# One fused kernel on one core: the output projection in three products of split parts, the mask counted ahead of the context, and a new order for every engine

## The reference, cut to what matters

```python
# L0: a routed low-rank update; lora_A is the context, 4 matrices of 64 rows
w     = softmax(x @ router_W.T + router_b)
a_sum = einsum('bsh,arh->bsr', x, lora_A)
x     = nan_to_num(x + 0.5 * einsum('bsn,bsnh->bsh', w, einsum('bsr,nhr->bsnh', a_sum, lora_B)))
# L1: cross attention, 32 heads of 16, over the 64 context rows; masked rows are left out
Q, K, V = x @ Wq.T + bq, ctx @ Wk.T + bk, ctx @ Wv.T + bv
scores   = where(mask != 0, Q K / 4, -inf)
attn_out = (softmax(scores) @ V) @ Wo.T + bo        # "the output projection"
x = layernorm(x + attn_out) * ln_g + ln_b
# L2 and L3, the same function: the 8 nearest of 512 columns, then 4 blocks
for i in range(4):
    p = leaky_relu(x); g = p gathered at the 8 neighbours
    x = (W_i @ p + (W_i @ g).sum(neighbours)) / 9 + x
```

## Time and profile before

| | us |
|---|---|
| median of 3 runs | 396.26 (395.89 to 396.88) |
| the profiled execution's own time | 396.18 |
| its span in the trace | 394.4 |
| PE busy | 379.3 (96%) |
| DVE busy | 274.2 (70%) |
| ACT busy | 173.8 (44%) |
| POOL busy | 122.8 (31%) |

### The profile page before, as it was taken

The page is one execution under the profiler, slowest core; times in us unless marked ns, Lnnn a source line. Parts: engine busy times, 40 slices in busy tenths (PEclk is TensorE's granted clock), DMA queues, the critical chain, the costliest instruction groups (busy, mean ns, idle before and its releaser), DMA issues.

```text
span 394.4 us, 6512 instructions
## 1 busy us (share of the span) xinstructions
PE 379.3 (96%) x2396; PEld 306.0 (78%) x2396; DVE 274.2 (70%) x410; ACT 173.8 (44%) x297; POOL 122.8 (31%) x116
## 2 busy tenths in 40 slices
PE   8899997998999989999999999999999999999996
PEld 7567786863976666666768988998899889988995
DVE  3968749689269874573779988785768564667764
ACT  1375438465467845454444433433433342333421
POOL 7560030210020313041413574452445231343420
PEclk9999999999999999999999999999999999999999
DMA  7994113407235303500000000000000001000012
GB/s 199 322 354 141 55 39 93 90 2 175 60 107 136 69 7 74 134 2 0 2 1 2 2 0 2 0 2 0 2 1 2 0 2 53 2 0 2 0 55 106
DMA packets 25199, 22.60 MB, mean 57 GB/s; under 512 B 9553, under 2 KB 20689, under 8 KB 25169
## 3 DMA queue, kind: packets, MB, share of 16 engines
q1 hardware_dynamic: 24496, 22.17, 20.6%
q10 hardware_dynamic: 672, 0.02, 0.1%
HBM read 12.48 MB, written 3.15 MB: 40 GB/s over the span
## 4 chain that ended last, share of the span: by engine, by line
PE 82%; DVE 6%; SPq 4%; ACT 3%; issue 2%; DMA 2%; POOL 1%; ACTq 0%; DVEq 0%; POOLq 0%
PE slot L537 79%; SPq L431 4%; DVE shift L1199 2%; DMA mask_col_i<-in_maskT 2%; ACT probT L929 2%; DVE x L1182 1%; PE slot L660 1%; PE slot L692 1%; POOL q_lo L1018 1%; DVE x L1184 1%; SPq L456 0%; PE slot L651 0%; DVE kT_lo L1135 0%; ACT L929 0%; DVE scratch L1183 0%
## 5 line engine op out<-in xcount | busy, mean ns | idle before, releaser
L1018 POOL TENSOR_TENSOR p_lo<-p_full,p_hi 128x512 fp32r<-128x512 f32 x64 | 87.9, 1383 | 148.7 <-ACT p_hi L969 148.3
L969 ACT ACTIVATE p_hi<-p_full 128x512 fp32r<-128x512 f32 x64 | 40.1, 631 | 81.8 <-DVE p_full L1257 81.8
L537 PE MATMUL slot<-adj,u_hi 128*128 128x512 f32 x256 | 71.4, 401 | 0.0
L537 PE MATMUL slot<-adj,u_lo 128*128 128x512 f32 x256 | 70.3, 397 | 0.0
L1262 DVE TENSOR_TENSOR u_lo<-slot,u_hi 128x512 fp32r<-128x512 f32 x64 | 43.3, 687 | 37.2 <-ACT u_hi L979 36.9
L537 PE MATMUL slot<-fs_hi,p_hi 128*128 128x256 f32 x256 | 64.8, 286 | 0.8 <-ACT probT L929 0.8
L537 PE MATMUL slot<-fs_lo,p_hi 128*128 128x256 f32 x256 | 63.9, 282 | 0.0
L1267 DVE SCALAR_TENSOR_TENSOR points<-slot,points 128x512 f32<-128x512 f32 x64 | 43.9, 687 | 28.4 <-PE slot L537 28.0
L1257 DVE SCALAR_TENSOR_TENSOR p_full<-points 128x512 f32<-128x512 f32 x64 | 59.9, 946 | 4.2
L979 ACT ACTIVATE u_hi<-slot 128x512 fp32r<-128x512 f32 x64 | 38.0, 598 | 56.1 <-PE slot L537 55.9
L537 PEld LDWEIGHTS slot<-adj,u_hi 128*128 128x128 f32 x256 | 45.5, 189 | 10.7 <-issue 2.9
(11 more groups left out here) (130 smaller groups left out, 531.3 us busy)
## 6 DMA issues: line engine op xcount, KB each, us to landing
q_stack<-q_hi SPq DMA_DIRECT2D x32, 128.0 KB, 2.4
x_in<-in_xT SPq DMA_DIRECT2D x8, 256.0 KB, 4.8
q_stack<-q_lo SPq DMA_DIRECT2D x16, 128.0 KB, 3.0
out_points<-points SPq DMA_DIRECT2D x8, 256.0 KB, 2.0
loraB_raw<-in_lora_BT SPq DMA_DIRECT2D x1, 1024.0 KB, 8.1
wk<-in_WkT SPq DMA_DIRECT2D x1, 1024.0 KB, 10.8
wq_raw<-in_WqT SPq DMA_DIRECT2D x1, 1024.0 KB, 11.3
wv<-in_WvT SPq DMA_DIRECT2D x1, 1024.0 KB, 11.5
```

The lines of the kernel that those rows point to most:

```text
L537: return pe.matmul(dst, lhsT, rhs, start=start, stop=stop, skip_group_check=True)
L969: act.activation(p_hi[b][:, (i % 2) * H:(i % 2 + 1) * H], p_full[:, p_buf[b, i]], ACT.Copy)\
L1018: pool.tensor_tensor(lo[:, cut], full[:, cut], hi[:, cut].bitcast(F32), ALU.subtract)\
```

## The change

There are four edits.

**Output projection.** `wo` is loaded as `wo_raw`. ACT rounds it to `wo_hi` (step `woh`), POOL subtracts for `wo_lo` (step `wol`). `wo_hi` lies in the room of the adjacency matrix of batch 3 and `att_hi` in a part of that of batch 2, so both matrices are now copied (`adjC2`, `adjC3`) only after `oc3`. For each batch and half, ACT rounds `attT` to `att_hi` (`ah`) and DVE subtracts for `att_lo` (`al`). Each matmul of 128 x 512 in 32 bits becomes three in fp32r.

**Mask.** `fm` is cut in two: `fa` counts the mask and now stands first on DVE, ahead of `a_ready`. The mask is loaded first.

**Loads.** Their order is a list of names. The small biases are now issued ahead of `wq`.

**Orders.** All five lists are new; the numbers of banks and buffers too.

```diff
+LOADS = "mask ctxT x0 xyz0 loraB wk xyz1 x1 small wq wv wo"
 PE_STEPS = """
...
 DVE_STEPS = """
-a_ready fm near0_0 near0_3 near0_1 near0_2 rA0 rB0 mk kl ml0_0 ml0_1 near1_0 rA1 init rB1 near1_1 raw0_0 near1_2
+fa init a_ready fm rA0 near0_2 near0_0 near0_3 near0_1 rB0 near1_0 ml0_0 ml0_1 near1_1 rA1 rB1 raw0_0 nan0_0 kl vr
...
-        wo = sb("wo", [P, KC, H])
+        wo_raw, = under(("wo_raw", [P, KC, H], F32))
+        wo_lo = sb("wo_lo", [P, KC, H], F32R)
...
-        attT = sb("attT", [P, KC, S])
+        attT, = under(("attT", [P, KC, S], F32))
+        att_lo = sb("att_lo", [P, KC, S], F32R)
...
+        att_hi = adj[:, 2, 0:2].rearrange("p m (t s) -> p (m t) s", s=S)
+        wo_hi = adj[:, 3]
...
-                elif kind == "oa":
-                    after(pe, att_ready, "dv", b, 0)
-                    loaded(pe, "wo")
-                    for t in range(ST):
-                        for k in (0, 1):
-                            mm(bank("rows", b, 0, t), attT[:, k, t * P:(t + 1) * P], wo[:, k, :], False, False)
...
+                elif kind in ("oa", "ob", "oc"):
+                    if kind == "oa":
+                        pe.wait_ge(wo_lo_ready, KC)
+                    after(pe, att_lo_ready, "al", b, 0 if kind == "oa" else 1)
+                    for t in {"oa": (0, 1), "ob": (0,), "oc": (1,)}[kind]:
+                        for k in (0, 1) if kind == "oa" else (2, 3):
+                            for step, (aa, ww) in enumerate(((att_hi, wo_hi), (att_hi, wo_lo), (att_lo, wo_hi))):
+                                last = mm(bank("rows", b, 0, t), aa[:, k, t * P:(t + 1) * P], ww[:, k, :],
+                                          False, step == 2 and k == KC - 1)
...
+                elif kind == "woh":
+                    loaded(act, "wo")
+                    act.activation(flat(wo_hi), flat(wo_raw), ACT.Copy).then_inc(wo_hi_ready, 1)
+                elif kind == "ah":
+                    after(act, att_ready, "dv", b, i)
+                    if b >= 1:
+                        after(act, output_done, "oc", b - 1)
+                    act.activation(half_of(att_hi, i), half_of(attT, i), ACT.Copy).then_inc(att_hi_ready, 1)
                 elif kind == "adjC":
+                    if b >= 2:
+                        after(act, output_done, "oc", B - 1)
                     after(act, turned_done, "adjT", b)
...
+                elif kind == "wol":
+                    pool.wait_ge(wo_hi_ready, 1)
+                    low_part(flat(wo_lo), flat(wo_raw), flat(wo_hi), KC, wo_lo_ready)
...
+                elif kind == "al":
+                    after(dve, att_hi_ready, "ah", b, i)
+                    dve.tensor_tensor(half_of(att_lo, i), half_of(attT, i), half_of(att_hi, i).bitcast(F32),
+                                      ALU.subtract).then_inc(att_lo_ready, 1)
```

More of the change, by code:

```diff
@@ L71 @@
-gb3_6 wd2_7 gc3_6 ga2_7:1,2 gd3_6 gb2_7 wa0_7:0,3,1 gc2_7 wb0_7 gd2_7 wc0_7 wa3_7:1,4,0 wd0_7 wb3_7 ga0_7:0,2 wc3_7
-gb0_7 wd3_7 ga3_7:3,5 gc0_7 gb3_7 gd0_7 gc3_7 gd3_7
+lora0:0 dist0_0:1 router0:0 dist0_1:2 dist0_2:3 dist0_3:4 keys:6,7 adjT0:2,3 mixed0:0,1 dist1_0:4 lora1:5 dist1_1:4
+ua0:0,2 router1:1 ub0 values:4,5 uc0 mixed1:3,0 dist1_2:1 qa0:2,4 dist1_3:5 ua1:3,6 qb0 ub1 qc0 lora2:5 sc0_0:0,1
+uc1 router2:7 sc0_1:2,3 rows0:0,1 sc0_2:4,5 sc0_3:2,3 qa1:6,4 adjT1:2,3 shift0:5 dist2_0:7 qb1 mixed2:2,3 qc1
@@ new lines @@
+sc1_0:6,7 lora3:5 ua2:2,3 w0_0:4,5 sc1_1:6,7 ub2 w0_1:4,5 sc1_2:6,7 uc2 at0_0:4,5,2 at0_1 w0_2:6,7 router3:3
+w0_3:6,7 at0_2 sc1_3:6,7 at0_3 dist2_1:3 qa2:6,7 shift1:3 qb2 norm0:2,3 qc2 mixed3:4,5 dist2_2:2 oa0 sc2_0:2,3
+ua3:6,4 w1_0:2,3 ub3 w1_1:2,3 uc3 sc2_1:2,3 ob0 sc2_2:6,7 oc0 sc2_3:2,3 at1_0:6,7,5 dist2_3:4 w1_2:2,3 at1_1
+w1_3:2,3 at1_2 shift2:4 at1_3 qa3:2,3 norm1:6,7 rows1:0,5 qb3 qc3 oa1 ob1 oc1 w2_0:2,3 sc3_0:0,1 w2_1:6,7 sc3_1:4,5
+wa0_0:2,3,0 at2_0:0,1,6 wb0_0 w2_2:4,5 wc0_0 at2_1 wd0_0 w2_3:4,5 at2_2 ga0_0:2,7 sc3_2:4,5 gb0_0 at2_3 gc0_0
@@ L464, in _, with load_first @@
-            load(b_all[:], ln_b.unsqueeze(0).broadcast_to([P, H]), "ln")
+            def load_first(name):
+                if name == "ctxT":
+                    load(ctx_t[:], chunks(ctxT), name)
+                elif name == "mask":
+                    src = mask.rearrange("b v -> (b v)").unsqueeze(0).broadcast_to([P, B * V])
+                    load(mask_all_i[:], src, "mask_all")
+                elif name in ("x0", "x1"):
+                    load_x(int(name[1:]))
+                elif name in ("xyz0", "xyz1"):
+                    load_xyz(int(name[3:]))
+                elif name == "loraB":
+                    load(loraB_raw[:], chunks(lora_BT), name)
+                elif name == "wk":
+                    load(wk[:], chunks(WkT), name)
+                elif name == "wq":
+                    load(wq_raw[:], chunks(WqT), name)
+                elif name == "wv":
+                    load(wv[:], chunks(WvT), name)
+                    load(bv_all, bv.unsqueeze(0).broadcast_to([P, H]), "bv")
+                    for half in range(2):
+                        load(mask_col_i[half * V:(half + 1) * V, :], maskT, "mask_col")
+                elif name == "wo":
+                    load(wo_raw[:], chunks(WoT), name)
+                    load(g_all[:], ln_g.unsqueeze(0).broadcast_to([P, H]), "ln")
+                    load(b_all[:], ln_b.unsqueeze(0).broadcast_to([P, H]), "ln")
+                elif name == "small":
+                    load(bk_col[:], bk_cols, "bk")
+                    load(bq_col[:], bq_cols, "bq")
+                    sp.dma_start(bo_col[:], bo.rearrange("(c p) -> p c", p=P), allow_slow_non_contiguous=True)\
+                        .then_inc(loads["bo_col"], 16)
```

140 lines of the change are left out of this document (68 added, 72 removed).

## The result

The changed kernel takes 393.43 us in the median of 5 runs (391.98 to 394.08), the kernel before 395.89 on the same chip: a ratio of 0.9927, 95% interval 0.9901 to 0.9952. On a second chip it was 0.9944 (0.9924 to 0.9965). The forecast was 389.6 us: the direction was right, and the gain was 2.5 us where 6.7 was expected. The time lies in the range of 384.5 to 395.5.

A forecast was written before the change was run, and what follows sets the result against it. PE was taken as the bound, busy 379.3 of 394.4 us. From 396.18 us: -5.4 (products) +0.5 (`ob1`) -0.9 (start) -1.6 (50 to 100) +0.8 (tables) = 389.6 us, range 384.5 to 395.5.

The forecast's parts named there:

- Products: Output projection on PE: 96 fp32r matmuls at 0.23 us, 22.0 us in place of 27.4, saving 5.4 us.
- ob1: Batch 1's output projection: other DVE steps stand between its `dv` and `al`, 0.5 us lost.
- Start: Up to `ua0`, expected at about 27.7 us: net 0.9 us won, between 1.5 won and 2.0 lost.
- So it gives 0 by itself: Mask loaded and counted first on DVE: no gain or loss, as `fm` still ends ahead of `wk`.
- 50 to 100 us: PE lacks 4.9 us here; a third of it, 1.6 us, taken as won by the new order.
- Table loads: Two more on ACT, around batch 2's exponentials: 0.8 us lost, between 0 and 2.9.
- rival 4: A drain follows each table load: 4.8 us more, 394.4 us; chance 0.08 together with another rival.
- From 200 us on: Same work in pairs of batches, same last seven steps: 0 us change, the last 3.1 us stay.
- Rival 2: Gain eaten: PE has less work but waits more between products; 396.2 us, chance 0.10.
- Rival 3: Chain `dv`, `ah`, `al` stands bare before `oa` and `ob`: slower, 401.5 us or so, chance 0.09.

The follow-up runs named there:

- e2: The changed kernel with the output projection back in 32 bits, new orders kept; ratio to the kernel before 1.0038.
- e1: The changed kernel timed again with no edit; ratio to the kernel before 0.9944, median 393.33 us.
- e13: The change with mask third and counted late, third product using `att_hi` for `att_lo`, `al` steps removed; ratio to the kernel before 0.9898.
- e7: The change with the mask still loaded first but counted behind `a_ready`; ratio to the kernel before 0.9916.
- e9: The change with the mask loaded third and counted after `a_ready`, as before; ratio to the kernel before 0.9873.
- e12: Edit on e10: `w0_2` moved ahead of `at0_1` and `gd0_1` ahead of `at3_0`, useful PE work for two waits; ratio to the kernel before 0.9935.
- e10: Edit on e9: ACT rounds the side weights (`fh`) behind batch 1's exponentials; ratio to the kernel before 0.9898.
- e6: Edit on e10: square root `dev1` moved behind batch 2's exponentials, saving two table loads; ratio to the kernel before 1.0053.
- e3: The kernel before, its orders and loads kept, with only the three products' steps inserted; ratio to the kernel before 1.0228.
- e11: Edit on e10: five products of no use put in PE's wait behind `w0_2`; ratio to the kernel before 0.9944.

## Why the forecast missed, point by point

**Products, -5.4: right.** The cadence is 0.23, and the change's profile shows no wait for the low part beyond 0.2 us (forecast 0.5 for `ob1`). e2 against e1 gives 3.7 us of time, 4.6 with the clock taken off, with an error of about 1 on either. e13 leaves room for 1 us or so in the `al` steps, which with the 4.6 would reach the 5.4 of the cadence; that sum is not shown.

**Start, -0.9 with `ua0` at 27.7: wrong, by 1.9 us.** This is the step that failed first: that "`a_ready` waits behind it, and `fm` still ends at about 14, ahead of `wk` at 15.59. So it gives 0 by itself". It looked at what the count delivers and not at what is queued behind it: `a_ready` on DVE, and every load behind the broadcast on the queue. The forecast named `a_ready` as waiting and did not follow it to `lora0`: it took the count to be done before the context lands, and then nothing is lost. In the profile the count ends at 8.3, while in e7, where `a_ready` waits for the context alone, that lands at 7.3, itself 2.3 us later than in before. `lora0` starts at 9.54 instead of 7.67 and `wk` lands 1.9 us later. e9 has `ua0` at 27.55, so the rest of the start's term was right where nothing else held it up. In time the edit costs about 1.6 us: the three ratios without it have a mean of 0.9895, the two with it 0.9936. Of the 1.6, up to 1.1 is the clock (mean loss 2.2 with it, 1.2 without).

**50 to 100 us, -1.6: mis-sized.** Measured by PE's lack: 0.5 won. The third was a guess between wide ends, and by the forecast's own words no row stood behind it. e12 and e10 suggest why it was too much: filling one wait moved it or won nothing.

**Table loads, +0.8: the sign fits, the size was too large.** The load at 138.25 stands ahead of the exponentials as one did in before; the two extra ones are those at 141.68 and 145.12:

```profile
138.25 1.28 ACT L966 ACT_TABLE_LOAD   x1
...
140.71 0.39 PE L561 MATMUL slot<-fs_hi,p_hi 128*128 128x256 f32 x1 [0.53 <-ACT probT L966]
...
141.68 1.28 ACT L981 ACT_TABLE_LOAD   x1
...
145.12 1.28 ACT L966 ACT_TABLE_LOAD   x1 [1.85 <-PE slot L561]
...
147.58 0.62 PE L561 MATMUL slot<-q_stack,k_stack 100*128 100x256 f32 x3 [0.88 <-ACT probT L966]
```

PE waits 0.53 and 0.88 us for these exponentials, 1.4 together, where before it waited 1.23: 0.2 more. From 100 to 200 us PE lacks 1.5 more in all, near the 1.3 that the forecast had for `ob1` and the tables together, but from other places: waits of 0.2 to 0.5 us spread over the stretch. That the total fits is luck. The drain of rival 4 did not show: the square root starts 0.02 us behind its load in e6 above.

**From 200 us on, 0: right.**

**The clock: not in the sum at all.** The forecast read "at a granted clock of 0.9 or more in every slice" as a property of the kernel. It was one of one execution, and 17 executions of the change have a mean loss of 2.2 us against 0.75 in before.

The account against 389.6, in the two profiled executions: the start is 1.9 worse than forecast, 50 to 100 us 1.1, 100 to 200 us 0.2, and PE's own work 0.7 better (6.1 saved against 5.4). That makes 2.5; the profile, at 391.98, shows 2.4. The median adds 1.45. The clock can account for it (its loss in the other four executions is 1.6 to 3.6), but so in part can the loads: in e1's profile `wk` landed 1.5 us later, and executions of before at the full clock vary from 394.9 to 397.2. No run separates the two in the median. Rival 2, the gain eaten by waits, is seen in the 3.0 us that PE lacks more, two thirds of them at the start and not between products. Rival 3 is seen at work in e3, but the new lists keep it away.

What stays open: what decides whether a given wait is followed by the lower clock. Waits of 1.1 us at the same place brought it in some executions and not in others, and e11 did not lower the loss. Longer waits brought it more often. In seven profiles PE waits 1.86 to 3.76 us before the keys, and in six of them the lower clock follows within 3 us of the keys' start; in the twelve in which that wait is 0.48 to 1.72 us it does not.

## What to carry to other kernels

An instruction moved to the head of an in-order engine or queue is priced by what stands behind it: follow each such step to the first instruction of the bound engine. Where engines pass work to each other in turn, book nothing for filling one wait until the next one's release has been read. And compare the mean clock over many executions, not in one profile: a version that waits longer in one piece can lose twice.
